# The order of VectorE's maxima, subtractions and addition in a decoder's two small-head attentions, and the bank of the output product

## What is computed

```python
x = layernorm(x + self_attention(x, w_qkv, w_proj, b_proj))      # no mask
x = layernorm(x + cross_attention(x, ctx, ctx, Wq, Wk, Wv, Wo, bo))  # causal mask
# per head: softmax(q k^T * 8**-0.5) v, then the output product and its bias
```

## Time and profile before

| | us |
|---|---|
| runs | 1648.48, 1644.72, 1644.19; median 1644.72 |
| the profiled execution | 1647.15 |
| its span, first to last instruction | 1645.1 |
| busy in the span: TensorE, VectorE, ScalarE, GpSimd | 1559.6, 1227.5, 916.7, 676.9 |
| the two attentions' pipeline | from 5 to 317 of the span |

### The profile page before, as it was taken

The page is one execution under the profiler, slowest core; times in us unless marked ns, Lnnn a source line. Parts: engine busy times, 40 slices in busy tenths (PEclk is TensorE's granted clock), DMA queues, the critical chain, the costliest instruction groups (busy, mean ns, idle before and its releaser), DMA issues. The chain is left out here.

```text
span 1645.1 us, 57105 instructions
## 1 busy us (share of the span) xinstructions
PE 1559.6 (95%) x20644; PEld 1301.3 (79%) x20644; DVE 1227.5 (75%) x3513; ACT 916.7 (56%) x2620; POOL 676.9 (41%) x1068
## 2 busy tenths in 40 slices
PE   7998999899999999999999999899999999999795
PEld 5776777687777777777777777699999999999664
DVE  6888888677777777777777677478888888888654
ACT  5776777643554444554444455566666666666251
POOL 3666655411233333333333333234444444444446
PEclk9999999999999999999999999999999999999997
DMA  3214221111221000000000110122222122122231
GB/s 106 67 44 115 77 57 53 49 55 41 61 64 28 26 26 26 26 26 26 26 26 27 29 28 25 30 58 54 53 63 59 45 63 58 46 63 59 76 111 38
DMA packets 157664, 82.44 MB, mean 50 GB/s; under 512 B 17642, under 2 KB 153116, under 8 KB 157569
## 3 DMA queue, kind: packets, MB, share of 16 engines
q1 hardware_dynamic: 154800, 77.68, 17.7%
q0 software_dynamic: 2048, 3.15, 0.6%
q10 hardware_dynamic: 720, 0.33, 0.1%
HBM read 61.03 MB, written 21.27 MB: 50 GB/s over the span
## 5 line engine op out<-in xcount | busy, mean ns | idle before, releaser
L1492 PE MATMUL bank<-diff_xT,diff_w_score 128*128 128x128 f32 x2048 | 256.4, 278 | 0.7 <-ACT diff_xT L1609 0.7
L1492 PEld LDWEIGHTS bank<-diff_xT,diff_w_score 128*128 128x128 f32 x2048 | 238.7, 192 | 22.4 <-issue 20.2
L1616 ACT ACTIVATE diff_keys<-bank 128x512 f32<-128x512 f32 x256 | 152.4, 595 | 161.6 <-PE bank L1492 161.6
L2095 ACT ACTIVATE lat_prob<-bank,lat_neg_max 128x128 f32<-128x128 f32 x512 | 181.1, 367 | 89.5 <-DVE lat_neg_max L2250 88.0
L1806 POOL TENSOR_TENSOR diff_prob<-diff_prob,diff_inv_sum 128x512 f32<-128x512 f32 x64 | 67.1, 1049 | 369.9 <-DVE diff_inv_sum L1709 369.9
L2312 POOL TENSOR_TENSOR lat_prob<-lat_prob,lat_inv_sum 128x512 f32<-128x512 f32 x128 | 133.4, 1042 | 147.8 <-DVE lat_inv_sum L2232 146.9
L2018 PE MATMUL bank<-lat_catT,lat_query 128*128 128x128 f32 x1024 | 138.9, 279 | 2.3 <-ACT lat_query L2106 2.1
L1986 PE MATMUL bank<-lat_catT,lat_w_score 128*128 128x128 f32 x1024 | 137.9, 278 | 3.2 <-issue 2.6
L2006 PE MATMUL bank<-lat_w_vo,lat_ctxT 128*128 128x128 f32 x1024 | 130.3, 275 | 1.1 <-ACT lat_ctxT L2118 1.1
L1986 PEld LDWEIGHTS bank<-lat_catT,lat_w_score 128*128 128x128 f32 x1024 | 124.4, 192 | 4.9 <-issue 4.0
L2018 PEld LDWEIGHTS bank<-lat_catT,lat_query 128*128 128x128 f32 x1024 | 124.5, 192 | 4.7 <-ACT lat_query L2106 3.7
(11 more groups left out here) (274 smaller groups left out, 3644.2 us busy)
## 6 DMA issues: line engine op xcount, KB each, us to landing
lat_c_rep<-cat SPq DMA_DIRECT2D x128, 128.0 KB
stage<-low_y SPq DMA_DIRECT2D x64, 64.0 KB, 1.6
diff_x_rep<-stage SPq DMA_DIRECT2D x128, 32.0 KB, 1.8
lat_c_t<-cat SPq DMA_DIRECT2D x32, 128.0 KB, 2.1
exp_w<-in_L_ffn_w_dram SPq DMA_DIRECT2D x16, 256.0 KB
expert_rows<-latw_zeros SPq DMA_DIRECT2D x4, 548.0 KB, 6.4
exp_rows<-expert_rows SPq DMA_DIRECT2D x8, 274.0 KB
low_x_t<-in_x_dram SPq DMA_DIRECT2D x32, 64.0 KB, 1.9
```

The source lines that it names most:

```text
L1492: last = nc.tensor.matmul(ring[(k + d) % 2][:, j * P:(j + 1) * P], w_score[:, H1 * (k // 2) + HS * d + 4 * (k % 2) + j, :], xT[:, :], star ...
L1616: nc.scalar.activation(keys[:, k // 2, 4 * (k % 2):4 * (k % 2) + 4, :].rearrange("p h t -> p (h t)"), ring[(k + d) % 2][:, :], ACT.Copy).t ...
L2095: last = nc.scalar.activation(prob[:, q, m, :], ps_s[q][:, m * T:(m + 1) * T], ACT.Exp, bias=neg_max[:, q, m:m + 1], accum_out=row_sum[:, ...
```

## The change

VectorE takes the first and the second maximum, then the first and the second subtraction, then the addition to z; before, z stood between the two halves. The output product moves from bank 1 to bank 0, where the products of the keys and queries lie. New waits go with it: the keys' product waits for z of the slot before, the output product for ScalarE's copy of the keys, and z for ScalarE's copy of the queries. The attention product no longer waits for z; it waits for the normalisation and the copy of the turned attention output, which use bank 1. The feed-forward layer's first transposition waits for the last z rather than for the last queries.

```diff
--- before.py
+++ after.py
@@ -322,7 +322,7 @@
         ps_s = [core.bank[4 + g] for g in range(4)]
         L = S // 2
         ps_o = ps_tail[:, 0:VW * H0 // 2].rearrange("p (g e) -> p g e", e=VW)
-        ps_oT, ps_out = ps_tail[:, 2 * P:3 * P], ps_tail[:, 3 * P:4 * P]
+        ps_oT, ps_out = ps_tail[:, 2 * P:3 * P], ps_qk[:, 2 * P:3 * P]
 
         def cross_weights():
 
@@ -394,6 +394,8 @@
                     pe.wait_ge(self.w_copied, 5)
                 wait(pe, self.xT_ready, i + 2)
                 wait(pe, self.qT_ready, i + 1)
+                if on(-3):
+                    wait(pe, self.z_done, i - 2)
                 kv = self.xT[:, w, :]
                 nc.tensor.matmul(ps_qk[:, P:2 * P], self.wk[:, w, :], kv, start=True, stop=True).then_inc(self.k_done, 1)
             if on(-1):
@@ -401,6 +403,8 @@
             if on(-2):
 
                 wait(pe, self.oT_ready, i - 1)
+                if on(1):
+                    wait(pe, self.kT_ready, i + 2)
                 nc.tensor.matmul(ps_out, self.oT[:, :], self.wo[:, int(cr(-2)), :], start=True, stop=True)\
                     .then_inc(self.out_done, 1)
             if on(1):
@@ -420,7 +424,8 @@
                 cross_weights()
             if on(-1):
 
-                wait(pe, self.z_done, i - 1)
+                wait(pe, self.onorm_done, i - 1)
+                wait(pe, self.oT_ready, i - 1)
                 if isinstance(i, int) and i == 1:
                     pe.wait_ge(self.w_copied, 10)
                 for hp in range(8):
@@ -497,7 +502,7 @@
         core, nc = self.core, self.nc
         ps_tail = core.bank[1]
         ps_o = ps_tail[:, 0:VW * H0 // 2].rearrange("p (g e) -> p g e", e=VW)
-        ps_out = ps_tail[:, 3 * P:4 * P]
+        ps_out = core.bank[0][:, 2 * P:3 * P]
 
         def take_weights(w, src, count):
 
@@ -510,12 +515,19 @@
                     self.wv[:, w, odd, :].rearrange("p (g o e) -> p g o e", o=2, e=HD0)[:, :, odd, :],
                     src[2].rearrange("p (g o e) -> p g o e", o=2, e=HD0)[:, :, odd, :]).then_inc(self.w_copied, 1)
 
-        def shift(i, par, c):
-
-            half = core.psum[:, 4 + 2 * c:6 + 2 * c, 0:4 * S].rearrange("p g (h t) -> p g h t", h=4)
-            top = self.row_max[:, par, 8 * c:8 * c + 8].rearrange("p (g h) -> p g h", g=2)
+        def views(par, c):
+            return (core.psum[:, 4 + 2 * c:6 + 2 * c, 0:4 * S].rearrange("p g (h t) -> p g h t", h=4),
+                    self.row_max[:, par, 8 * c:8 * c + 8].rearrange("p (g h) -> p g h", g=2))
+
+        def highest(i, par, c):
+
+            half, top = views(par, c)
             wait(dve, self.s_done, 2 * i + 1 + c)
             nc.vector.tensor_reduce(top, half, AX.X, ALU.max).then_inc(self.max_done, 1)
+
+        def shift(i, par, c):
+
+            half, top = views(par, c)
             if c == 0:
 
                 wait(dve, self.t_done, 2 * i - 2)
@@ -549,14 +561,17 @@
                 nc.vector.tensor_scalar(self.rstd[:, 1 - par, :], self.mean_var[:, 1 - par, 1:2], EPS, None, ALU.add)\
                     .then_inc(self.veps_done, 1)
             if on(0):
+                highest(i, par, 0)
+                highest(i, par, 1)
                 shift(i, par, 0)
+                shift(i, par, 1)
             if on(-2):
 
                 wait(dve, self.zb_done, i - 1)
                 wait(dve, self.out_done, i - 1)
+                if on(1):
+                    wait(dve, self.qT_ready, i + 2)
                 nc.vector.tensor_tensor(self.z[:, par, :], self.z[:, par, :], ps_out, ALU.add).then_inc(self.z_done, 1)
-            if on(0):
-                shift(i, par, 1)
             if on(-2):
                 wait(dve, self.z_done, i - 1)
                 nc.vector.bn_stats(self.stats[:, par, :], self.z[:, par, :]).then_inc(self.stats_done, 1)
@@ -888,7 +903,7 @@
                                                 w_out[:, t, :], start=(t == 0), stop=(t == NT - 1))
                 last.then_inc(self.out_done, 1)
 
-        pe.wait_ge(self.low.qT_ready, NI)
+        pe.wait_ge(self.low.z_done, NI)
         self.slots(pe, slot, between)
         self.drain(pe, slot)
 
```

## The result

The changed kernel took 1643.31 us (median of 20 runs, 1637.42 to 1646.75), the kernel before 1645.99 us (20 runs, 1644.19 to 1650.04): a ratio of 0.9974, 95% interval 0.9965 to 0.9984. The ratio is of the means, 1642.4 and 1646.6 us; the medians are 2.7 us apart.

A forecast was written before the change was run, and what follows sets the result against it. The prediction took a loop of TensorE and VectorE, with a 0.28 us pause in each, to bound the slot. Gains of 4.7, 6.5, 1.1, 1.9 and 2.0 made 16.2 us, from 1644.72 to 1628.5; range 1621 to 1640.

The forecast's parts named there:

- TensorE's release: Scores follow the attention product after 0.68 us instead of 1.04, a gain of 0.36 a slot at most.
- VectorE's order: Maxima, subtractions and z in steps of 0.61 us; VectorE needs 3.72 a slot against 3.96, no bound in plain slots.
- its wait: On VectorE, z waits for the queries' copy and starts at 3.46 us, with 0.60 to spare before the scores are due.
- ScalarE didn't limit: ScalarE as new limit in self attention: slot not surely under 3.98 us, so 0.31 gain taken, between 0.26 and 0.36.
- loop through z: Rival C, slower: queries' copy, z, normalisation and transposition form a loop; 6 us more, 1651; chance 0.04.
- Weight-step slots: Eight written-out slots with feed-forward weight steps on VectorE gain 0.24 us each, 1.9 in all.
- The output product waits for the keys' copy: In TensorE's queue, the output product goes ahead of the queries' product; values' products still start at 125.03; cost nothing.
- the cover: The values' products' 0.19 us wait for the transposed probabilities' copy hides the later queries' product; without it, 0.19 to 0.22 a slot.
- rival B: The cover fails: values' products pushed by up to 0.22 us, 0.05 to 0.15 a slot remain, around 1638; chance 0.17.
- iteration ends: At 11 loop iteration ends, TensorE's way back limits the gain to 0.1 us each, bounds 0 and 0.51; 1.1 in all.
- written-out slots: Outside the loops: eight with weight steps gain 0.24 us each, ten others 0.2 each; 1.9 and 2.0 in all.

The follow-up runs named there:

- e5: The e1 kernel with one wait put back: the output product also waits for the keys' copy; 1646.38 us, ratio 0.9993 to the kernel before.
- e2: The kernel before with one edit: the output product also waits for the keys' copy; 1666.13 us, ratio 1.0099.
- e1: The changed kernel with the output product in the unused half of bank 6, without its wait for the keys' copy; 1634.32 us, ratio 0.9915 to the kernel before.
- e3: VectorE's new order alone against the kernel before, output product still in bank 1, attention product waiting for z; 1639.11 us, ratio 0.9956.
- e10: VectorE's order alone, output product in bank 1, run again on one chip with e9 and e11; 1637.92 us, ratio 0.9954 to the kernel before.
- e7: The kernel before with the cross attention loop in 3 iterations of 8 slots instead of 6 of 4; 1658.68 us, ratio 1.0063.
- e11: The bank 6 kernel of e1 again, on one chip with e9 and e10; 1633.98 us, ratio 0.9932 to the kernel before.
- e9: The changed kernel once more, unaltered, on one chip with e10 and e11; 1642.99 us, ratio 0.9982 to the kernel before.
- e6: The changed kernel with the cross attention loop in 3 iterations of 8 slots instead of 6 of 4; 1654.18 us, ratio 1.0032 to the kernel before.

## Why the prediction was wrong

**What held.** TensorE's release: the scores start 0.72 us after the attention product, where 0.68 was taken from the earlier trace rows, and VectorE's subtraction is out of the way. VectorE's order: steps of 0.60, where 0.61 was forecast; two steps that waited on their forerunner had taken 0.72 and 0.79. The sentence of the Trainium skill that the prediction set against this ("VectorE: DVE Perf Modes", section "The DRAIN you can't avoid"), that chaining without semaphores gains nothing, doesn't hold for these rows. The same section also says that a next operation which isn't held starts earlier, and with that the 0.60 agrees; the prediction had left it out. z starts at 3.38 (forecast 3.46), and e5 shows that its wait is free in a plain slot. ScalarE didn't limit, nor did any loop through z. Weight-step slots: from slot 28 to slot 36 the gain is 1.0 where 1.9 stood, but two profiles of the same code differ there by 1.3, so this term is neither borne out nor refuted.

**The step that failed: "The output product waits for the keys' copy ... I cost this at nothing".** In a plain slot the values' and the attention products start 0.22 later for it, of the 0.32 that the release brings (e2: 0.23 later; e5 against e1: 0.20). The working had three errors in one direction, 0.05, 0.07 and 0.10. The output product starts 0.15 after the copy's end (125.64 to 125.79), where the queries' had started at 0.10 (124.49 to 124.59). The queries' product follows it by 0.29, not 0.22. The two weight loads are still 0.22 apart (125.75 and 125.97), but the first product follows its load by 0.04 and the second by 0.11; in the rows that gave 0.22 it was the second of the two that had just waited. And the values' products follow the queries' by 0.32, not 0.22; that distance was never seen free in the trace before, where the wait lay over it. The idle 0.19 in front of the values' loads was not all slack: in the changed kernel 0.13 are idle there (126.27 to 126.40) though nothing holds them. Counted from product to product, the cover was what 0.44 (124.59 to 125.03) leaves over 0.32, so 0.12, not 0.19. With 2.30 for the old start of the queries' product after the scores (122.29 to 124.59), the sum 2.30 + 0.05 + 0.29 + 0.32 is the 2.96 measured. The prediction had named this as rival B with a chance of 0.17, and even its price, 12 to 14 us; e5 puts the wait at 12 to 13, of which about 10 are the wait's own by the stretches. What it never priced is the other half of the choice: VectorE's order with the output product left in bank 1, which does without that wait and was faster (e3, e10).

**The second step: iteration ends, "I take 0.1".** The reading was right, TensorE's way back sets the start there (1.19 before, 1.23 after), and the row was in the earlier trace rows. What was missing is that such a slot also gains nothing to set against a later attention product: it lost 0.19 in self attention (4.42 to 4.61) and 0.21 to 0.26 in cross attention. The slot behind it gained 0.03. With two plain slots at 0.10, a self iteration gained 0.05 (17.23 to 17.18) and a cross iteration nothing (18.95 to 18.92 or 18.97), where the prediction had 1.03 and 1.18. By the table above the cross loop gained 0.15 in six iterations, the last four self iterations 0.76, of which 0.34 in slot 12 alone. Of the 16.2 us of the sum 12.2 stood in the loops (5 x 1.03 + 6 x 1.18), and 0.9 came, less 2.3 lost in the first iteration, where the prediction had no term. The written-out slots, where 4 us stood, gained 0.75 + 1.00 + 1.20, about 3, in these two profiles; against e7's slots 0 to 8 and 28 to 36 the first two would be losses. Only the last is seen in every profile (13.4 us against 14.6 and 14.3). What the change might have given with the first step right, e11 shows nearly: 12.7 us in the pipeline (294.36 to 281.70), a self iteration 16.46 for 17.23 and a cross iteration some 18.1 for 18.95.

**In between.** Rival B was the case that came. Its own estimate, 0.05 to 0.15 left a slot, fits the plain slots (0.10), but not the ends.

**Open.** In the first iteration of the self loop TensorE stood still for 1.90 us, and nothing that the profile shows released it:

```profile
59.42 0.14 PEld L380 LDWEIGHTS bank<-ident,low_x_t 128*128 128x128 f32 x1 [1.90 <-issue]
```

That iteration took 19.62 us against 17.30 before (17.90 in e7), 20.18 and 19.09 in e9 and e6, 20.07 in e5, 18.76 and 17.23 in the two profiles of the bank 6 kernel, 17.91 and 17.56 with the order alone. So all three profiles of the changed kernel lose there against both of the kernel before, by 1.2 to 2.9 us. Fetching of the loop's code is a guess that wasn't tested.

## What to carry to other kernels

A wait that is moved ahead of an instruction in a busy queue costs more than the wait: what stood in its shadow must now run behind it, at distances that may differ from those read elsewhere, and the cover is only what the next wait leaves over such a distance. Read those distances where the instruction isn't held, or count them as unknown, and work out every kind of slot apart; here plain, iteration-end and cross slots gave three different answers. Price each half of a two-part change alone: here one half gave more than both. And look for a buffer that is idle for another engine's reason before sharing one that needs a wait in the tight queue: the output product in the half-empty bank 6 gave over three times the gain of the one in bank 0 (1 - 0.9915 against 1 - 0.9974; on one chip 1 - 0.9932 against 1 - 0.9982).

## What was not expected of the hardware

- At the end of a loop iteration TensorE took 1.18 to 1.27 us from its attention product to the next scores in the kernel before and in the changed one, though plain slots had gone from 1.04 to 0.72 between them. In the bank 6 kernels it was 1.29 to 1.40; why they take more is open.
- A loop body of 8 slots instead of 4 raised that to 4.5 to 4.9 us, with 24 packets in the instruction queue instead of 4, and made three kernels 9 to 10 us slower each.
- Two products of 128 x 128 in float32 were 0.22 us apart in the kernel before and 0.29 in the changed one, where the first had just waited; from such a product to the 32-column ones it was 0.31 to 0.32 where nothing held them.
